# Last attention group of a decoder layer: heads and transposed probabilities by pairs of token tiles, and one row maximum moved ahead on VectorE

## The reference

```python
x = x + _L0_attn_ref(_layernorm(x))        # attention over the batch axis
x = x + _L0_xattn_ref(_layernorm(x), ctx)  # cross attention: 32 query heads, 8 KV groups, head size 128
x = x + _L0_ffn_ref(_layernorm(x), ...)    # top-4 of 16 experts, and a shared expert
```

```python
q = (hidden_states @ Wq.T); k = (ctx @ Wk.T); v = (ctx @ Wv.T)     # q and k are RMS-normalised
scores = jnp.einsum('bhqd,bhkd->bhqk', q, k) * scale + mask
probs = jax.nn.softmax(scores, axis=-1)
out = jnp.einsum('bhqk,bhkd->bhqd', probs, v)
return out @ Wo.T
```

## Time and profile before

| | |
|---|---|
| time, median of 3 runs | 843.34 us (842.74 to 844.18) |
| the profiled execution: time, and span of the core | 843.19 us, 841.4 us |
| TensorE busy | 807.9 us (96%) |
| VectorE busy | 525.6 us (62%) |
| ScalarE busy | 503.9 us (60%) |
| GpSimd busy | 529.7 us (63%) |
| chain that ended last, by engine | PE 69%, POOL 9%, DVE 6%, issue 5%, DMA 5%, ACT 3% |
| the last group's stretch | about 526 to 574 us |

### The profile page before, as it was taken

How to read it: one execution, slowest core, us unless ns; L and a number is a source line. 1 busy time by engine, 2 the same in 40 slices (tenths; PEclk the granted TensorE clock), 3 DMA queues, 4 the chain that set the end, 5 groups by cost and what they waited for, 6 DMA issues and landing times.

```text
span 841.4 us, 19340 instructions
## 1 busy us (share of the span) xinstructions
PE 807.9 (96%) x6801; PEld 451.5 (54%) x6801; DVE 525.6 (62%) x965; ACT 503.9 (60%) x954; POOL 529.7 (63%) x442
## 2 busy tenths in 40 slices
PE   6789999999999999999999999899999999999997
PEld 2664645645645645645645645545455555555553
DVE  6797886586586586587487487796943222222237
ACT  3798987586587586586586686354234443433431
POOL 6953496796797797797787787722434344444431
PEclk9799999999999999999999999999999999999999
DMA  8029426326326326326336334355165576688933
GB/s 327 6 90 284 153 86 233 109 96 213 117 90 233 101 94 229 101 95 229 100 102 222 101 110 154 114 226 176 27 240 189 171 251 219 229 298 280 398 129 150
DMA packets 51739, 142.47 MB, mean 169 GB/s; under 512 B 6368, under 2 KB 8416, under 8 KB 47328
## 3 DMA queue, kind: packets, MB, share of 16 engines
q1 hardware_dynamic: 43568, 116.93, 41.5%
q0 software_dynamic: 7520, 24.65, 8.2%
q10 hardware_dynamic: 592, 0.08, 0.1%
HBM read 97.85 MB, written 41.68 MB: 166 GB/s over the span
## 4 chain that ended last, share of the span: by engine, by line
PE 69%; POOL 9%; DVE 6%; issue 5%; DMA 5%; ACT 3%; SPq 2%; DVEq 0%; POOLq 0%; ACTq 0%
PE ps L1683 36%; PE ps L2146 5%; PE ps L2148 5%; PE ps L2147 5%; PE ps L2125 2%; POOL ring_mem L618 2%; PE ps L2169 2%; PE ps L2170 2%; PE ps L2171 2%; DMA stage<-in_wq 2%; PE ps L1904 2%; POOL reg_h L656 2%; POOL ring_mem L604 2%; POOL reg_h L660 2%; PE ps L1890 1%
## 5 line engine op out<-in xcount | busy, mean ns | idle before, releaser
L1683 PE MATMUL ps<-wo_hi,reg_b 128*128 128x512 f16 x448 | 142.4, 379 | 1.0 <-DVE x_res L1319 0.8
L697 POOL DMA_INDIRECT y_rows<-reg_h,to_row x47 | 48.8, 1039 | 112.3 <-ACT reg_h L1105 107.1
L656 POOL TENSOR_SCALAR reg_h<-reg_h 128x512 f32<-128x512 f32 x56 | 94.3, 1684 | 30.4 <-ACT reg_h L907 30.1
L660 POOL TENSOR_TENSOR reg_h<-reg_h 128x512 f16<-128x512 f32 x84 | 108.7, 1294 | 4.7
L1683 PE MATMUL ps<-hT_hi,wq_hi 128*128 128x512 f16 x256 | 97.1, 379 | 0.6 <-DVE ring_mem L1262 0.4
L1683 PE MATMUL ps<-hT_lo,wq_hi 128*128 128x512 f16 x256 | 97.0, 379 | 0.0
L1683 PE MATMUL ps<-hT_hi,wq_lo 128*128 128x512 f16 x256 | 97.0, 379 | 0.0
L618 POOL TENSOR_TENSOR ring_mem<-kv,ring_mem 128x512 f16<-128x512 f32 x64 | 80.3, 1254 | 23.5 <-ACT ring_mem L832 23.5
L1683 PE MATMUL ps<-wo_lo,reg_b 128*128 128x512 f16 x224 | 84.9, 379 | 0.0
L1093 ACT ACTIVATE reg_h<-ps 128x256 f32<-128x256 f32 x47 | 18.0, 384 | 90.2 <-PE ps L2148 90.2
L2146 PE MATMUL ps<-ring_mem,reg_h 128*128 x188 | 71.3, 379 | 0.1
(11 more groups left out here) (337 smaller groups left out, 2017.2 us busy)
## 6 DMA issues: line engine op xcount, KB each, us to landing
ring_mem<-w_split SPq DMA_DIRECT2D x16, 1536.0 KB, 7.5
w_split<-reg_h SPq DMA_DIRECT2D x88, 256.0 KB, 2.1
reg_h<-in_wgu SPq DMA_DIRECT2D x58, 256.0 KB, 3.3
stage<-in_wq SPq DMA_DIRECT2D x8, 1024.0 KB, 8.0
stage<-in_wo SPq DMA_DIRECT2D x8, 1024.0 KB, 6.0
reg_h<-in_wd SPq DMA_DIRECT2D x30, 256.0 KB, 3.1
wkv_st<-in_wkv SPq DMA_DIRECT2D x8, 512.0 KB, 8.7
ring_mem<-in_x_half SPq DMA_DIRECT2D x8, 256.0 KB, 5.7
```

What stands on the lines that cost most here:

```text
L656: pool.tensor_scalar(st, st, WS, None, ALU.mult).then_inc(pre_scaled_pool, 1)
L660: pool.tensor_tensor(hl[:, 1, :], st, hl[:, 0, :], ALU.subtract).then_inc(pre_split, 1)
L697: pool.indirect_dma_start(y_rows, bass.IndirectOffsetOnAxis(ap=to_row[:, r - 1:r], axis=0), y[r % 2], None).then_inc(scattered[r % 2], 16)
L1683: last = pe.matmul(dst, lhsT(c), rhs(c), start=(m == 0), stop=(m == n - 1))
```

## The change: what it does

In the last group `transpose_probs`, `heads_out`, `probs_hi`, `heads_hi`, `probs_lo` and `heads_lo` are replaced by the pair forms that the other groups use, and the six functions go. The pairs 0 and 2 stand ahead of the loop over tiles, the transposes of pair 4 and 6 at t = 1 and 3, their heads at t = 2 and 4. On VectorE the fourth row maximum, `row_max(i, 3)`, moves from behind the first `add_output` to ahead of the second normalisation; the low part of the second half of v moves behind `add_output(i - 1, NT - 1)`.

```diff
@@ ScalarE, iteration
                     if att and not proj and k == 2:
-                        probs_hi(i, 0)
-                        probs_hi(i, 1)
+                        pair_probs_hi(i, 0)
                     if att and not proj and k == 3:
-                        heads_hi(i, 0)
+                        pair_heads_hi(i, 0)
+                    if att and not proj and k == 4:
+                        pair_probs_hi(i, 2)
+                        pair_heads_hi(i, 2)
...
                 for t in range(NT if att or split else 0):
-                    if att and proj and t in (2, 4):
+                    if att and t in (2, 4):
                         pair_heads_hi(i, t + 2)
...
-                    if att and not proj and t + 2 < NT:
-                        probs_hi(i, t + 2)
+                    if att and not proj and t in (1, 3):
+                        pair_probs_hi(i, t + 3)
...
-                    if att and not proj and t + 1 < NT:
-                        heads_hi(i, t + 1)
@@ VectorE, iteration, not proj
                     row_max(i, 2)
-                    probs_lo(i, 0)
-                    probs_lo(i, 1)
+                    pair_probs_lo(i, 0)
+                    row_max(i, 3)
                     normalise(i, 1)
-                    heads_lo(i, 0)
+                    pair_heads_lo(i, 0)
                     add_output(i - 1, NT - 2)
-                    row_max(i, 3)
+                    pair_probs_lo(i, 2)
+                    add_output(i - 1, NT - 1)
                     v_lo_part(i, 1, 5)
-                    add_output(i - 1, NT - 1)
+                    pair_heads_lo(i, 2)
                     normalise(i, 2)
...
-                    if att and proj and t in (2, 4):
+                    if att and t in (2, 4):
                         pair_heads_lo(i, t + 2)
...
-                    if not proj and t + 2 < NT:
-                        probs_lo(i, t + 2)
-                    if not proj and t + 1 < NT:
-                        heads_lo(i, t + 1)
+                    if not proj and t in (1, 3):
+                        pair_probs_lo(i, t + 3)
@@ TensorE, iteration, att and not proj
                     output(i - 1, NT - 2, wo_hi, wo_lo)
-                    transpose_probs(i, 0)
-                    transpose_probs(i, 1)
-                    heads_out(i, 0)
-                    pe.wait_ge(scaled, 4 * i + 4)
+                    transpose_pair(i, 0)
+                    heads_pair(i, 0)
                     output(i - 1, NT - 1, wo_hi, wo_lo)
+                    transpose_pair(i, 2)
+                    heads_pair(i, 2)
                 if att:
                     for t in range(NT):
-                        if proj and t in (2, 4):
+                        if t in (2, 4):
                             heads_pair(i, t + 2)
...
-                        if not proj and t + 2 < NT:
-                            transpose_probs(i, t + 2)
-                        if not proj and t + 1 < NT:
-                            heads_out(i, t + 1)
+                        if not proj and t in (1, 3):
+                            transpose_pair(i, t + 3)
```

More of the change, by code:

```diff
@@ L838, in soft_exp @@
                 act.activation(prob[:, b, :], prob[:, b, :], ACT.Exp).then_inc(exp_done, 1)
[L840 to L848, removed]
             def pair_probs_hi(i, t):
@@ L1289, in normalise @@
                                   ALU.mult).then_inc(prob_done, 1)
[L1291 to L1301, removed]
             def pair_probs_lo(i, t):
@@ L1855, in sum_k_squares @@
                 pe.matmul(ps[:, bank, :], ones[:, :], ksq_lo[:, th, :], start=False, stop=True).then_inc(ssq_k_ps, 1)
-            def transpose_probs(i, t):
-                b = t // 2
-                if t % 2 == 0:
-                    pe.wait_ge(prob_done, ev(i, 4, b))
-                if t >= 2:
-                    pe.wait_ge(pT_split, ev(i, NT, t - 2))
-                for m in range(2):
-                    col = ((t % 2) * 2 + m) * P
-                    last = pe.transpose(ps[:, 6 + t % 2, m * P:(m + 1) * P], prob[:, b, col:col + P], ident[:, :])
-                last.then_inc(pT_ps, 1)
-            def heads_out(i, t):
-                pe.wait_ge(pT_split, ev(i, NT, t))
-                if t == 0:
-                    pe.wait_ge(scaled, 4 * i + 4)
-                else:
-                    pe.wait_ge(o_split, ev(i, NT, t - 1))
-                for n, (v, pt) in enumerate(((v_hi, pT_hi), (v_hi, pT_lo), (v_lo, pT_hi))):
-                    for r in range(2):
-                        rows = slice(r * S, (r + 1) * S)
-                        last = pe.matmul(ps[:, r, 0:256], v[rows, t, :], pt[rows, t, :],
-                                         start=(n == 0), stop=(n == 2))
-                last.then_inc(pv_ps, 1)
             def transpose_pair(i, t):
```

## The result

The changed kernel takes **846.31 us** (median of 22 runs, 843.56 to 856.83), the kernel before 843.37 in the same comparison (22 runs, 840.77 to 853.54): a ratio of **1.0033**, 95% interval 1.0018 to 1.0049. It is slower by some 2.9 us, and the predicted time (845.7) and range (843.2 to 847.4) held. The stages show that two terms were missing from the sum, of opposite sign. The profiled execution took 846.38 us, with a span of 844.6 for 841.4.

The account below looks back on a forecast made before the run. In the last group TensorE and VectorE were both taken as the bound, VectorE setting the pace. Turns -0.80 and hand-offs +3.25 gave +2.45 on 843.34, about 845.7 us; range 843.2 to 847.4.

Parts of the forecast that it names:

- Fewer turns: TensorE, last group: pairs switch less often between kinds of work, a gain of 0.80 us.
- the five forecast waits: TensorE, last group: 1.58, 1.57, 1.51 before first heads, second heads, third transposes; 0.50, 0.88 before token transposes.
- Fewer instructions on VectorE: VectorE, last group: four pairs save 0.32 us of its time, next to nothing for the total.
- Longer hand-offs: TensorE, last group: waits for pair splits total 6.04 us for 2.79 before, a loss of 3.25.
- The sum, +2.45: Whole change: -0.80 for turns and +3.25 for hand-offs, giving about 845.7 us.
- The row maximum: VectorE, ahead of the second normalisation: its 0.60 us lies in idle time near 541.89 and costs nothing.
- Rival 3: TensorE's stop at 582.27 falls elsewhere or goes, worth 0.96: +1.5 in all, 844.8 us; chance 14%.
- the forecast is wrong if the stop near 582 has gone: Sign against the forecast: TensorE's 1.50 us stop behind the logits, expected to stay, disappears.

Follow-up runs that it names:

- e4: Kernel before with pairs in tiles 0 to 3 of the last group and the row maximum moved, single tiles behind; ratio 1.0043 to the kernel before.
- e3: Changed kernel plus five unread matmuls on TensorE between the first pair's transposes and heads; 42.79 us from the group's first to last token transposes.
- e9: Changed kernel with output(i - 1, 7) moved ahead of the first heads, behind the first pair's transposes; ratio 1.0028 to the kernel before.
- e2: Kernel before with pairs in tiles 4 to 7 of the last group alone, row maximum where it was; ratio 0.9996 to the kernel before.
- e1: Kernel before with only the fourth row maximum moved ahead of the second normalisation, single tiles kept; ratio 0.9998 to the kernel before.
- e11: e4 once more, unchanged, for a second profile; run once, 849.27 us.
- e10: The kernel before once more, unchanged, for a second profile; run once, 845.62 us.
- e8: Changed kernel with 16 already fulfilled waits on TensorE between the first pair's transposes and its heads; ratio 1.0042 to the kernel before.
- e7: The changed kernel once more, unchanged, for a second profile; run once, 848.28 us.

## Why the prediction was right, and where its sum was not

**Fewer turns, -0.80: held.** e4's pair heads take 0.76 from start to start and its `output(i - 1, 7)` starts at 538.86, the predicted time. In e3, the changed order at full clock, A less the five forecast waits (6.40 from start to start) is 36.39, for 40.19 - 2.79 = 37.40 before: -1.01, of which the turns are about the forecast -0.80 and 0.17 was not forecast: the token transposes ahead of the shared expert's unit take 0.45 to the next start for 0.62 (at 572.93 in e3, 569.98 before).

**Fewer instructions on VectorE, 0.32: held.** 0.61 and 1.14 against two times 0.31 and 0.60 are 0.01 + 0.06 per pair, 0.28 for four. By the Trainium skill's rule (Perfetto Trace Analysis, section Optimizing Scalar/DVE Operations: some 125 ns of overhead per VectorE instruction on PSUM) it would be 1.0 us (an estimate); the trace shows about a quarter of that.

**Longer hand-offs, +3.25: held, a little small.** Counted from start to start, as the prediction did, the new waits of TensorE are 1.71, 1.65, 1.53, 0.59 and 0.92, together 6.40 for 6.04 predicted, each longer than its forecast by 0.02 to 0.13. Less the 2.79 of before they are +3.61. The predicted starts were 538.10, 543.52 and 548.39. In the changed kernel they are 538.27, 545.40 and 550.29, of which 1.6 in the last two is the clock; in e3, whose clock stayed up, the distances from the first transposes are 7.71 and 12.60 for 7.49 and 12.36 predicted. VectorE's idle times were predicted as 0.90 and 0.98, measured as 0.82 and 0.92 in e3, and as 1.87 (with the slow output in it, and 0.48 ahead of it) and 0.92 in the changed kernel. The sum, +2.45, has its counterpart in e3: -1.01 + 3.61, A = 42.79, **+2.60**; e9 has the same A. The mechanism and its size are shown, and e2 and e4 put it into the first four tiles: the split of a pair comes back only when both tiles are through ScalarE and VectorE, and at the head of the group no other step of TensorE's program lies in between to cover the wait.

**The row maximum, 0: held,** as far as it was tested. The prediction said that its 0.60 would lie in VectorE's idle time and would cost as much without that. In e1 VectorE has no idle time there, and it cost nothing either: the row maximum stood ahead of the third normalisation before as well.

**Missing: the granted clock, +1.6.** The prediction took every matmul at its length at full clock and named no term for the clock, although a wait of 1.58 us in front of the heads was its main result. In the changed kernel the granted clock was 0.50 behind that wait in both profiles, 44.41 for e3's 42.79. It was left out because the kernel before showed 1.00 in this stage, with no wait longer than 1.00 us.

**Missing from the sum, though a rival: the stop, -0.94.** Rival 3 (14%) said that the stop at 582.27 could fall elsewhere or go with fewer instructions ahead, and would be worth 0.96; it went, and B fell from 8.85 to 7.91. It did not come with 844.8 us, because the clock took 1.6 in the same execution. So the forecast +2.4 met a measured difference of 2.9 in the medians and 3.2 in the profiled executions; the latter is made of +2.6, +1.6 and -0.94, and that the medians are made of the same parts is not shown. The range held for a good reason (the hand-offs) and for a lucky one (two missing terms of opposite sign, which leave +0.7). By the prediction's own test, "the forecast is wrong if the stop near 582 has gone", one of its steps was wrong.

**What stays open.** Why the clock falls in one execution and not in the next of the same program (e4, e11) was not settled; nor how often it does in executions that were not profiled. Executions differ outside of the stage too: e10 took 845.62 us for 843.19 with A and B as before. With intervals that reach 1.3 us or more to either side, the medians cannot resolve terms of a microsecond. Nor is it settled why the packet comes either about 3.7 us after the last token transposes or by up to 3.9 us earlier, with nothing between but e2's 1.1: it may be where a block ends among the instructions, or a place in a queue behind the last store of `h_rows`, whose traffic ends some 3.5 us after the last token transposes in all thirteen profiles, just ahead of the packet in the eight late cases. No version beat the kernel before by more than a measurement can tell; e2 (0.9996) is its equal.

## What to carry to other kernels

Pairing the steps of a pipeline saves turns and instruction overhead (a pair saved 0.20 us of TensorE's time and 0.07 of VectorE's here) and nearly doubles the length of each hand-off; before pairing, look at what lies between the producer's step and its use. Where a whole output lies there, as in the last four tiles, the longer waits took only what the fewer turns gave (+0.48 and -0.49); where the consumer stands waiting, as in the first four, the longer hand-off comes through in full. A filling that is longer than the wait delays the next hand-off: e9's output of 2.69 us in a wait of 1.71 gained nothing. A new wait of 1.5 us or more on TensorE should be given a second, possible price, that of the matmuls behind it at half clock, and a stop on "issue" should be treated as something that any change of the number of instructions can move: compare stages, not only totals.

## What was not expected of the hardware

- **Half clock after a short wait.** Behind waits of 0.91 to 2.14 us TensorE's granted clock was 0.50 for some 3.4 us in each of six profiles, with matmuls back to back for nearly all of it, and cost 1.3 to 1.6 us (43.74 for 42.46 in one program, 41.70 for 40.19 with 16 waits more, 44.41 for 42.79). The same program did it in one execution and not in the other, and a wait of 2.60 us passed without it (e9). Behind stops of 1.49, 1.85 and 2.15 us it fell too (e1, e8, e3), and behind two of 1.50 it did not.
- **A late block of instructions.** The stop ends some 2.3 us after a packet of the instruction queue (0.02 MB), in eight profiles of eight. The Trainium skill (Runtime: NRT & Kernel Launch, section Instruction fetch mechanics) has such fetches mostly hidden; here five profiles agree, and so do the packets at 559.5 and 583.3 of the kernel before, beside which TensorE does not stop; in eight profiles one block was a stop of 1.05 to 2.15 us. A stop of this kind can be told by "issue" as what ended it, and by its place, which moved by the number of instructions ahead of it.
- **VectorE beside GpSimd.** A product of two SBUF operands took 1.57 us on VectorE in the changed kernel (1.12 was the longest the prediction knew, 0.69 the usual length), while GpSimd's L682 ran from 564.08 to 565.23; e3, e7 and e9 show the same 1.57. That GpSimd is the cause was not tested. It moved nothing visible: TensorE does not wait again before the last token transposes.

```profile
564.21 1.57 DVE L1315 SCALAR_TENSOR_TENSOR wo_lo<-ring_mem,wo_hi 128x512 f16<-128x512 f32 x1
```
